# Moving part of the weighting and adding of the down products from VectorE to ScalarE and GpSimd in a fused macaron block (feed-forward, attention, feed-forward) on one core

## The reference

```python
x = x + 0.5 * ffn(layernorm(x))
x = x + attention(layernorm(x))     # 8 sequences of 256, 16 query heads, 4 key heads, causal
x = x + 0.5 * ffn(layernorm(x))

def ffn(x):                          # 8 experts, top-p weights w, every expert over every token
    probs = softmax(x @ router_w.T); w = top_p_weights(probs, 0.9)
    for e in range(8):
        y = (silu(x @ gate_w[e].T) * (x @ up_w[e].T)) @ down_w[e].T
        out = out + y * w[:, e:e + 1]
```

## Time and profile before

| | |
|---|---|
| median of 3 runs | 1108.98 us (1108.06 to 1111.28) |
| the profiled execution | 1108.69 us |
| its span, first to last instruction | 1107.0 us |
| PE busy | 1087.7 us, 98% |
| DVE busy | 853.8 us, 77% |
| POOL busy | 641.0 us, 58% |
| ACT busy | 546.2 us, 49% |
| mean granted TensorE clock | 0.996 |

### The profile page before, as it was taken

How to read it: one execution, slowest core, us unless ns; L and a number is a source line. 1 busy time by engine, 2 the same in 40 slices (tenths; PEclk the granted TensorE clock), 3 DMA queues, 4 the chain that set the end, 5 groups by cost and what they waited for, 6 DMA issues and landing times.

```text
span 1107.0 us, 21233 instructions
## 1 busy us (share of the span) xinstructions
PE 1087.7 (98%) x7624; PEld 657.0 (59%) x7624; DVE 853.8 (77%) x1810; ACT 546.2 (49%) x1027; POOL 641.0 (58%) x673
## 2 busy tenths in 40 slices
PE   6899999999999999999999999999999999999998
PEld 4466656565665655566566566656656566666655
DVE  7988788767878887889888789888888765644443
ACT  4545554333555655645655555555555553333332
POOL 4545343346668677778677678586686643322332
PEclk8999999999999999999999999999999999999999
DMA  5311120010133333323333523443243320000000
GB/s 191 127 58 57 58 82 1 1 25 20 35 67 63 61 60 68 58 49 67 65 56 53 86 41 61 74 84 61 49 68 59 78 57 6 6 20 1 1 1 20
DMA packets 166008, 57.96 MB, mean 52 GB/s; under 512 B 158096, under 2 KB 162704, under 8 KB 165904
## 3 DMA queue, kind: packets, MB, share of 16 engines
q1 hardware_dynamic: 165904, 56.61, 24.7%
HBM read 15.70 MB, written 2.10 MB: 16 GB/s over the span
## 4 chain that ended last, share of the span: by engine, by line
PE 79%; DVE 3%; POOL 3%; issue 1%; DMA 1%; ACT 0%; DVEq 0%; ACTq 0%; POOLq 0%; SPq 0%
PE YB L358 25%; PE G L339 25%; PE U L339 24%; PE S L448 2%; PE S L431 1%; PE S L413 1%; PE S L459 1%; POOL room L1090 1%; POOL HS L1006 1%; DMA QKT<-room 1%; DVE TS L625 0%; DVE X L646 0%; ACT TS L500 0%; POOL RR L1063 0%; PE S L358 0%
## 5 line engine op out<-in xcount | busy, mean ns | idle before, releaser
L1006 POOL TENSOR_TENSOR HS<-TS,HS 128x512 f16<-128x512 f32 x256 | 300.7, 1176 | 394.8 <-ACT HS L507 394.1
L358 PE MATMUL YB<-W,HS 128*128 128x256 f16 x3036 | 373.4, 273 | 7.0 <-DVE X L646 4.6
L339 PE MATMUL G<-XS,W 128*128 128x512 f16 x1536 | 374.7, 380 | 0.3 <-ACT XS L533 0.3
L339 PE MATMUL U<-XS,W 128*128 128x512 f16 x1536 | 373.5, 379 | 0.0
L358 PEld LDWEIGHTS YB<-W,HS 128*128 128x128 f16 x3036 | 292.0, 98 | 89.4 <-DVE X L646 8.8
L507 ACT ACTIVATE HS<-TS 128x512 f16<-128x512 f32 x256 | 161.0, 629 | 320.5 <-DVE TS L630 319.3
L625 DVE SCALAR_TENSOR_TENSOR TS<-TS,G 128x512 f32<-128x512 f32 x256 | 174.8, 683 | 136.8 <-ACT TS L500 134.9
L500 ACT ACTIVATE TS<-G,TSC 128x512 f32<-128x512 f32 x256 | 175.1, 684 | 189.6 <-PE G L339 186.5
L339 PEld LDWEIGHTS U<-XS,W 128*128 128x128 f16 x1536 | 150.4, 98 | 181.7 <-issue 0.8
L339 PEld LDWEIGHTS G<-XS,W 128*128 128x128 f16 x1536 | 146.2, 98 | 131.9 <-issue 4.1
L630 DVE SCALAR_TENSOR_TENSOR TS<-TS,U 128x512 f32<-128x512 f32 x256 | 175.9, 687 | 27.8 <-DVE TS L625 0.5
(11 more groups left out here) (168 smaller groups left out, 759.1 us busy)
## 6 DMA issues: line engine op xcount, KB each, us to landing
room<-in_gate SPq DMA_DIRECT2D x4, 512.0 KB, 4.0
room<-in_up SPq DMA_DIRECT2D x4, 512.0 KB, 4.0
room<-in_down SPq DMA_DIRECT2D x4, 512.0 KB, 3.9
QKT<-in_gate SPq DMA_DIRECT2D x4, 512.0 KB, 4.8
QKT<-in_up SPq DMA_DIRECT2D x4, 512.0 KB, 4.0
QKT<-in_down SPq DMA_DIRECT2D x4, 512.0 KB, 4.7
out_y<-X SPq DMA_DIRECT2D x16, 128.0 KB, 1.8
X<-in_x SPq DMA_DIRECT2D x3, 512.0 KB, 6.9
```

Source lines behind the costliest of these rows:

```text
L339: mm = eng.matmul(bank[:, :], W[:, e, wl, jj, kk * I + m * P:kk * I + (m + 1) * P], flat(XS16[:, b % 2, xl, kk, :, :], 'cq'), start=q == 0 ...
L358: mm = eng.matmul(out, HS[:, j % 2, hl, kk, m * P:(m + 1) * P], W[:, e, wl, 2, kk * D:(kk + 1) * D], start=kk + hl + wl == 0, stop=kk == K ...
L1006: eng.tensor_tensor(HS[:, j % 2, 1, m, :], TS[:, k % 3, :], HS[:, j % 2, 0, m, :], ALU.subtract).then_inc(L['g_lo'].sem, 1)
```

## The change

Of the eighteen items of each attention period, eight (those whose slot 2k+10 is 2, 4, 10, 14, 20, 22, 30 or 34 slots after the period's start; `Y_ACT`, 64 items in all) are weighted by ScalarE, which reads YB and writes the product to a new tile YS (`act_y`), and GpSimd adds YS to X (`pool_y`). VectorE does the other 192 as before. Three helpers give the waits: `y_read` (YB may be overwritten), `x_added` (X holds the sum) and `y_weighted` (the weights are there). YS is one buffer: `act_y` waits for the `pool_y` before it. On both engines the new instruction stands directly behind the item's high or low part of the same slot.

With it some places change: the rotary sum `r` comes one slot earlier, the values' split `v` one slot later, the layernorm of odd tiles one slot earlier (-13 for -12), one transpose of the start goes from slot 2 to slot 4, and in the hand-written start GpSimd takes the second power and the low parts ahead of the router's conversions, ScalarE takes a high part ahead of a copy, and VectorE the small maximum `dve_wr0` ahead of a normalisation. Three one-column tiles now lie in MX0. The table of semaphores gets a lane `a_y` and a lane `g_y` (left out below).

```diff
@@ -70,13 +70,13 @@
...
-FTP0 = (0, 1, 2, 2)
+FTP0 = (0, 1, 2, 4)
...
-Q_STEP = {'qb': 1, 'rb': 1, 'sq': 1, 'ra': 2, 'ss': 2, 'rr': 4, 'r': 4, 'qn': 5, 'v': 6, 'qh': 6, 'ql': 7, 't': 8}
+Q_STEP = {'qb': 1, 'rb': 1, 'sq': 1, 'ra': 2, 'ss': 2, 'rr': 4, 'r': 3, 'qn': 5, 'v': 7, 'qh': 6, 'ql': 7, 't': 8}
...
@@ -85,7 +85,7 @@
...
-ATT, QKVP, OUTP = (by_tile(-24, -12), by_tile(-11, 1), by_tile(18, 42))
+ATT, QKVP, OUTP = (by_tile(-24, -13), by_tile(-11, 1), by_tile(18, 42))
...
@@ -97,6 +97,11 @@
...
+Y_SCALAR = (2, 4, 10, 14, 20, 22, 30, 34)
+Y_ACT = [k for k in range(NK) if 2 * k + 10 >= FIRST and 2 * k + 10 < FIRST + BATCH * (NB * BT // 2) and (2 * k + 10 - FIRST) % BATCH in Y_SCALAR]
+Y_DVE = [k for k in range(NK) if k not in Y_ACT]
...
@@ -151,6 +156,7 @@
...
         TS = sb('TS', [P, 3, BLK], F32)
+        YS = sb('YS', [P, D], F32)
...
@@ -202,7 +208,7 @@
...
-        BM, OSC, DSC = (sb(c, [P, 1], F32) for c in ('BM', 'OSC', 'DSC'))
+        BM, OSC, DSC = (MX0[:, c:c + 1] for c in range(3))
...
@@ -323,6 +329,27 @@
...
+        def y_read(eng, k):
+            if k in Y_ACT:
+                eng.wait_ge(*L['a_y'].at(Y_ACT.index(k), 'y'))
+            else:
+                eng.wait_ge(*L['v_y'].at(Y_DVE.index(k) if k >= 0 else k, 'y'))
+        def x_added(eng, k):
+            if k in Y_ACT:
+                eng.wait_ge(*L['g_y'].at(Y_ACT.index(k), 'y'))
+            else:
+                eng.wait_ge(*L['v_y'].at(Y_DVE.index(k) if k >= 0 else k, 'y'))
+        def y_weighted(eng, k):
+            j = k // 4
+            a, b, e = UNITS[j]
+            if j < BY_EXPERT:
+                eng.wait_ge(*L['v_wc'].at(j, 'wc'))
+            else:
+                eng.wait_ge(*L['v_wb'].at(NB * a + b - 2, 'wtc'))
...
@@ -344,9 +371,9 @@
...
-                eng.wait_ge(*L['v_y'].at(k - 1, 'y'))
+                y_read(eng, k - 1)
             elif ks[0] == 0:
-                eng.wait_ge(*L['v_y'].at(NK - 5, 'y'))
+                y_read(eng, NK - 5)
...
@@ -578,6 +605,15 @@
...
+        def act_y(eng, k):
+            j, m = divmod(k, 4)
+            a, b, e = UNITS[j]
+            n = Y_ACT.index(k)
+            eng.wait_ge(*L['p_y'].at(k, 'y'))
+            y_weighted(eng, k)
+            eng.wait_ge(*L['g_y'].at(n - 1, 'y'))
+            eng.activation(YS[:, :], YB[:, 0:D], ACT.Identity, scale=WTC[:, b, m, e:e + 1]).then_inc(L['a_y'].sem, 1)
         def act_slot(eng, s):
...
@@ -585,6 +621,8 @@
...
+                if (s - 10) // 2 in Y_ACT:
+                    act_y(eng, (s - 10) // 2)
             if s == W_FIRST['hi']:
...
@@ -634,11 +672,8 @@
...
-                if j < BY_EXPERT:
-                    eng.wait_ge(*L['v_wc'].at(j, 'wc'))
-                else:
-                    eng.wait_ge(*L['v_wb'].at(NB * a + b - 2, 'wtc'))
-            eng.wait_ge(*L['v_y'].at(k - 4, 'y'))
+                y_weighted(eng, k)
+            x_added(eng, k - 4)
...
@@ -808,7 +843,7 @@
...
             lane = L['v_al']
-            eng.wait_ge(*L['v_y'].at(4 * END[0, t // BT] + t % BT, 'y'))
+            x_added(eng, 4 * END[0, t // BT] + t % BT)
...
@@ -928,7 +963,8 @@
...
-                dve_y(eng, (s - 10) // 2)
+                if (s - 10) // 2 in Y_DVE:
+                    dve_y(eng, (s - 10) // 2)
...
@@ -1103,9 +1139,22 @@
...
+        def pool_y(eng, k):
+            j, m = divmod(k, 4)
+            a, b, e = UNITS[j]
+            n = Y_ACT.index(k)
+            eng.wait_ge(*L['a_y'].at(n, 'y'))
+            x_added(eng, k - 4)
+            if a and BEGIN[a, b] == j:
+                eng.wait_ge(*L['v_op'].at(b * BT + m, 'ad'))
+            x = X[:, b * BT + m, :]
+            eng.tensor_tensor(x, x, YS[:, :], ALU.add).then_inc(L['g_y'].sem, 1)
         def pool_slot(eng, s):
...
+                if (s - 10) // 2 in Y_ACT:
+                    pool_y(eng, (s - 10) // 2)
...
@@ -1149,7 +1198,7 @@
...
         def sp_store(eng, t, k):
-            eng.wait_ge(*L['v_y'].at(k, 'y'))
+            x_added(eng, k)
...
@@ -1282,11 +1331,16 @@
...
+            pool_f_xl(eng, 0)
+            pool_f_xl(eng, 1)
+            pool_f_xl(eng, 2)
...
-            pool_f_xl(eng, 0)
-            pool_f_xl(eng, 1)
+            pool_f_xl(eng, 3)
+            eng.wait_ge(*L['v_fep'].at(2 * BT - 1, 'eps'))
+            eng.wait_ge(*L['v_fx'].at(BT - 1, 'xn'))
+            eng.tensor_tensor(RSF[:, :], VEF[:, :], MH[:, 0:BT], ALU.pow).then_inc(L['g_frs'].sem, BT)
             lane = L['g_rw']
...
@@ -1298,11 +1352,6 @@
...
-            pool_f_xl(eng, 2)
-            pool_f_xl(eng, 3)
-            eng.wait_ge(*L['v_fep'].at(2 * BT - 1, 'eps'))
-            eng.wait_ge(*L['v_fx'].at(BT - 1, 'xn'))
-            eng.tensor_tensor(RSF[:, :], VEF[:, :], MH[:, 0:BT], ALU.pow).then_inc(L['g_frs'].sem, BT)
...
@@ -1313,9 +1362,9 @@
...
-            act_fc(eng, 1)
...
+            act_fc(eng, 1)
...
@@ -1334,8 +1383,8 @@
...
+            dve_wr0(eng, 0)
...
-            dve_wr0(eng, 0)
...

```

More of the change, by code:

```diff
@@ L228, in build @@
                 ('v_al', 'stats aggr eps'), ('v_ax', 'xn'), ('v_qb', 'qb'), ('v_ss', 'ss ms'), ('v_rb', 'rb r'), ('v_qn', 'qn'), ('v_ql', 'qlo klo'), ('v_mp', 'xa a xb b'), ('v_pv', 'rc rd ob'), ('v_op', 'ad'),
-                ('g_lo', 'lo'), ('g_w', 'lo2'), ('g_frs', 'rs'), ('g_fl', 'xl'), ('g_rk', 'eq b bp'), ('g_ars', 'rs'), ('g_al', 'xl'), ('g_ol', 'lo'), ('g_bo', 'bo'), ('g_sq', 'sq'), ('g_rr', 'rr sg'), ('g_ra', 'ra'), ('g_v', 'v1 r1 v2 r2 v3'), ('g_pl', 'a b'), ('g_rw', 'b1 r1 b2 r2 b3')]:
+                ('g_lo', 'lo'), ('g_w', 'lo2'), ('g_frs', 'rs'), ('g_y', 'y'), ('g_fl', 'xl'), ('g_rk', 'eq b bp'), ('g_ars', 'rs'), ('g_al', 'xl'), ('g_ol', 'lo'), ('g_bo', 'bo'), ('g_sq', 'sq'), ('g_rr', 'rr sg'), ('g_ra', 'ra'), ('g_v', 'v1 r1 v2 r2 v3'), ('g_pl', 'a b'), ('g_rw', 'b1 r1 b2 r2 b3')]:
             L[name] = Lane(sem(name), labels.split(), name in later)
```

## The result

In 20 executions each the changed kernel took 1110.61 us in the median (1109.68 to 1112.84), the kernel before 1108.94 (1107.96 to 1113.02): ratio 1.0015, 95% interval 1.0008 to 1.0021. It is slower, by little but measurably, where 1108.3 was forecast. The profiled execution has a span of 1109.0 us in 1110.69, against 1107.0 in 1108.69.

What follows compares the result with a forecast made beforehand. TensorE was taken as the bound, nearly without gaps. The terms -0.5 (wait at 352), -0.2 (near 260), -0.15 (start) and +0.2 (GpSimd) summed to about -0.7 us, a median near 1108.3 us, range 1105.8 to 1111.2.

Steps and rivals of the forecast that it cites:

- VectorE's relief, no gain but at the waits: Attention stage: VectorE loses 30.7 us of work, 538.3 to about 507.6, but TensorE gains only where it waits.
- The wait at 352: TensorE's 0.73 us wait at 352.46 for GpSimd's low part shrinks by about 0.5 us, the bias using earlier idle time.
- the step that ScalarE reads YB in time: Attention items: ScalarE's 64 added reads of YB cost nothing on the path, taken as 0, between 0 and +0.5 us.
- The wait near 260: Earlier layernorm and rotary sum reorder VectorE near 260 us: half of a 0.4 us wait gained, -0.2, between -0.4 and +0.4.
- The wait at 396 unchanged: The stage's longest wait, 0.91 us at 396.54, stays because none of its instructions is moved: gain 0, at best 0.9.
- The start: Reordered normalisations before the first gate product: -0.15 us, between -0.4 and +0.4.
- GpSimd, +0.2: 64 added adds on GpSimd, tight at a period's beginning with RR some 0.5 us late: +0.2 us charged for the whole.
- a repetition would cost up to 0.5 us more: Transposing DMA at a period's beginning: one late landing had cost 0.4 us; another would cost up to 0.5 more.
- A: Rival, chance 0.15: at a period's beginning GpSimd comes too late, RR late by 1.46 us, low part and DMA late: 1112.2.
- B: Rival, chance 0.10: the relief reaches all waits, those at 352 and 396 and short hidden ones too: 1105.8.
- D: Rival, chance 0.17: the change does nothing, instructions move and no wait changes: 1109.0.
- C: Rival, chance 0.13: a shifted start changes how much runs at TensorE's lower clock, up to 1.7 us either way: 1106.6 or 1110.0.

Runs made afterwards that it cites:

- e1: The changed kernel with no item moved, its new start and three shifted steps kept: 1111.03 us, ratio 1.0013 to the kernel before.
- e5: The changed kernel with the split of V put back one slot earlier, ahead of the second low part: 1109.94 us, ratio 1.0012 to the kernel before.
- e8: The kernel before with the new start alone, no item moved and the old steps: 1109.04 us, ratio 1.0003.
- e9: The kernel before with only two of the eight items moved, those around the squares and RR at a period's beginning: 1109.04 us, ratio 1.0002.
- e16: The changed kernel with 68 always-met waits added on VectorE, two in each of 34 slots: 1109.32 us, ratio 1.0000 to the kernel before.
- e13: The changed kernel with 18 always-met waits added on VectorE, one in each of 18 slots: 1110.56 us, ratio 1.0013 to the kernel before.
- e11: The kernel before with the split of V one slot later and nothing else: 1110.01 us, ratio 1.0010.

## Why the prediction was wrong

**VectorE's relief, no gain but at the waits: right.** Busy shares moved near to the forecast (GpSimd 493 against 500, ScalarE 377 against 387, the new instructions 459 and 764 ns against 470 and 700), save VectorE with 525 against 508: the term took 30.7 us of work away and asked of no remaining instruction what its new place would do to it (8.8 us more in e1).

**The wait at 352, -0.5 us: wrong, 0.** The low part came earlier, as said. The step that failed is "the split stays ahead of the second low part, so it gives nothing here": I asked what the moved split does for the low part, not what the low part now stands beside. It meets XN on VectorE (1.24 in place of 0.40 us) and the wait comes back as TensorE's for ScalarE's read of YB, 0.72 us. With it fell, at this one place, the step that ScalarE reads YB in time. e5 has the split back, its wait at this place is 0.22 us, just what was forecast, and it is 0.6 us faster.

**The wait near 260, -0.2 us: 0.** It went from 0.55 to 0.51 us. The term was half of a mean wait and named no mechanism.

**The wait at 396 unchanged: right in size**, 0.78 after, 0.91 before.

**The start, -0.15: right** within what can be measured (e8: -0.2 at a clock of 0.997, ratio 1.0003).

**GpSimd, +0.2: the step that cost most.** The term was sized by "RR starts near 523.7, some 0.5 us late". It was 1.49 late at three places: I had laid the first add on the idle time of 0.73 us, charged the second, and left the six other adds, the split and the bias out. The two alone make RR only 0.29 late (e9); together they overdraw the idle time. By itself that still cost little: in e16 RR is as late, and the kernel stands 0.3 us above the one before. What cost 1.4 us is what stood behind "a repetition would cost up to 0.5 us more": I took the median landing of 4.3 us for every landing and the late one for chance. Five of the 24 landings of the kernel before took 4.9 to 6.1 us, in the trace that I had, and each has a code packet beside it; the change moves those packets, since it changes how many instructions VectorE carries out. Both are needed at 696: with the old margin of 1.2 us a landing of 5.3 would not have been late, and a landing of 4.3 suffices with the thin margin (in e16 it ends 0.20 us ahead of the product, without a wait). At 402 the code packet alone did it.

**The sum.** Forecast -0.7, measured +1.6 at the same clock. Of the 2.3 between them 1.2 are what the code packets cost beyond the 0.2 that was charged, 0.5 the wait at 352 that changed its owner, 0.2 the wait near 260 that stayed. Some 0.4 are left and stay open; a part may be the down products at 528.53 and 686.91, which wait for the low part behind the late RR and took 1.62 us in place of 1.47.

**The rivals.** A named the right engine and a wait for QKT as its mark, and part of its margins, but not its mechanism: its wait was to return each period, and it came at two of eight, where code is loaded. B is excluded, since no relief reached a second wait. D is wrong in that waits did change. C's upper figure of 1110.0 is the nearest in time, by accident: at an equal clock the whole difference is there.

The Trainium skill has a rule that fits what the landings show: DMA: Bandwidth & Descriptors, section Queues, rings and completion order, says that a DMA engine takes turns between its queues packet by packet and finishes a packet before it changes. The 16 KB packets that began 3.0 to 4.1 us after the issue of a late landing took 0.9 to 1.0 us, and a landing with such a packet alone came 1.4 to 1.8 us late; why more than the packet's own time, no run shows.

## What to carry to other kernels

Edits that are each hidden by the same idle time of an engine have to be added up against it once, not one by one, and a moved instruction is to be asked what it now runs beside. A DMA whose landing varies is worth a look at what else its engines carry at that time: in this long unrolled program VectorE's code loads came with every 128th of its instructions, and adding or removing instructions moves all its later ones. So a change of 0.1% can be an effect of where code loads fall and not of the idea. Padding with waits that are always met can tell the two apart, with care: half of the waits here became no instruction of their own, e13 stayed slow for a reason not found, and 101 and 134 waits came with 0.5 to 1 us of time.

## What was not expected of the hardware

- A transposing DMA of the same size landed in 4.2 to 4.4 us in 114 of 144 cases. The 30 others took 4.8 to 6.7 us, and each had a packet of instruction code beside it.
- 68 waits that are always met, 34 more records on VectorE, made a kernel of 1110.5 us 1.4 us faster by shifting code loads.
- A normalisation of 128x256 on VectorE took 0.40 us beside GpSimd's short casts and 1.24 us beside GpSimd's 128x512 subtraction, which itself went from 1.16 to 1.20. The low part of the keys, 128x128, went from 0.43 to 0.87 us in the mean by a later place of GpSimd's split of the values alone (e11).
